# q and k stacked through a DRAM scratch, and the linear bias of the second block added by VectorE

## What is computed

```python
h = relu(layernorm(x))
q, k, v = h @ Wq.T, h @ Wk.T, h @ Wv.T + bv              # 12 heads of 32
scores = q . k * 384**-0.5 + (adj + adj)                  # rows of zeros only are masked
x = x + softmax(scores) v @ Wo.T + bo
h = relu(layernorm(x))
for l in range(2):
    u = h W_left[l] h^T (on and above the diagonal), h W_right[l] h^T (below), / sqrt(384)
    d = exp(u) * adj
    attention = d / (sum(d, axis=2) + 1e-10)
    h_lin = h @ W_lin[l].T + b_lin[l]
    ctx = attention @ h_lin
    h = relu(norm(ctx) * ln_a[l] + ln_b[l])
x = x + h
```

## Time and profile before

| | |
|---|---|
| median of 3 runs | 1622.85 us (1622.07 to 1628.5) |
| the profiled execution | 1625.41 us, span of its core 1623.7 us, mean granted TensorE clock 0.98 |
| busy of the span | PE 96%, PEld 94%, DVE 71%, ACT 57%, POOL 28% |
| last chain by engine | PE 87%, SyncE's queue 7%, DVE 2% |
| transfers | 76.19 MB, 116769 packets; q and k: 768 of 48 KB |
| one turn in the middle | 47.9 us |

### The profile page before, as it was taken

One profiled execution on the slowest core, in us unless ns is written; L12 is line 12 of the kernel. 1 busy time (PEld: TensorE's weight loads), 2 busy tenths in 40 slices (PEclk: granted clock), 3 DMA queues, 4 the chain that ended last, 5 costly groups with the idle time before them and its releaser, 6 DMA issues.

```text
span 1623.7 us, 39352 instructions
## 1 busy us (share of the span) xinstructions
PE 1550.8 (96%) x13888; PEld 1524.4 (94%) x13888; DVE 1146.9 (71%) x4303; ACT 922.7 (57%) x2155; POOL 457.1 (28%) x928
## 2 busy tenths in 40 slices
PE   3699999999999999999999999999999999999984
PEld 3699999999999999999999999999999999999974
DVE  5567777777777677776767777767777776777643
ACT  4456655566665566665556656555666655665632
POOL 4113222333232223322233323222332323332222
PEclk8789999999999999999999999999999999999996
DMA  6101112211112211112221111221111222111100
GB/s 212 40 21 41 43 50 54 53 44 31 47 44 50 54 50 30 42 44 50 53 54 43 33 45 44 50 53 50 33 40 42 53 50 53 46 30 46 31 11 20
DMA packets 116769, 76.19 MB, mean 47 GB/s; under 512 B 14282, under 2 KB 116432, under 8 KB 116576
## 3 DMA queue, kind: packets, MB, share of 16 engines
q1 hardware_dynamic: 116128, 73.06, 17.6%
q0 software_dynamic: 448, 0.60, 0.1%
HBM read 23.28 MB, written 12.58 MB: 22 GB/s over the span
## 4 chain that ended last, share of the span: by engine, by line
PE 87%; SPq 7%; DVE 2%; issue 1%; ACT 1%; DMA 1%; POOL 1%; DVEq 0%; ACTq 0%; POOLq 0%
PE bank L341 70%; SPq L297 6%; PE bank L417 5%; PE bank L347 4%; PE bank L410 3%; PE bank L401 3%; PE bank L423 1%; DMA k<-qk 1%; PE bank L435 0%; ACT prob L506 0%; DVE qk L599 0%; ACT qk L482 0%; SPq L304 0%; DMA x_sb<-x 0%; DVE weights L575 0%
## 5 line engine op out<-in xcount | busy, mean ns | idle before, releaser
L341 PE MATMUL bank<-h,weights 128*128 128x256 f32 x3456 | 429.9, 282 | 5.8 <-DVE h L740 5.1
L341 PEld LDWEIGHTS bank<-h,weights 128*128 128x128 f32 x3456 | 412.0, 190 | 6.7 <-issue 5.7
L506 ACT ACTIVATE prob<-prob,rmin 128x128 f32<-128x128 f32 x768 | 237.2, 404 | 49.9 <-DVE rmin L657 49.9
L341 PE MATMUL bank<-weights,h 128*128 128x384 f32 x1152 | 223.5, 338 | 0.0
L341 PE MATMUL bank<-hA,weights 128*128 128x256 f32 x1728 | 218.5, 283 | 1.4 <-DVE hA L599 1.4
L599 DVE TENSOR_TENSOR n<-bank,n 128x512 fp32r<-128x512 f32 x192 | 129.4, 687 | 122.8 <-ACT n L482 122.7
L341 PEld LDWEIGHTS bank<-hA,weights 128*128 128x128 f32 x1728 | 211.7, 190 | 1.7 <-DVE hA L599 1.7
L341 PEld LDWEIGHTS bank<-weights,h 128*128 128x128 f32 x1152 | 194.1, 188 | 0.0
L482 ACT ACTIVATE n<-bank 128x512 fp32r<-128x512 f32 x192 | 111.9, 606 | 113.9 <-PE bank L341 113.9
L657 DVE CUSTOM_DVE_ANT_0 prob<-bank,adj_sb 128x128 f32<-128x128 f32 x768 | 175.0, 287 | 0.2 <-issue 0.2
L482 ACT ACTIVATE qk<-bank 128x512 f16<-128x512 f32 x96 | 57.2, 595 | 170.5 <-PE bank L341 170.5
(11 more groups left out here) (107 smaller groups left out, 2652.2 us busy)
## 6 DMA issues: line engine op xcount, KB each, us to landing
q<-qk SPq DMA_DIRECT2D x384, 48.0 KB, 1.9
k<-qk SPq DMA_DIRECT2D x384, 48.0 KB, 2.0
x_sb<-x SPq DMA_DIRECT2D x32, 384.0 KB, 3.5
out<-x SPq DMA_DIRECT2D x32, 384.0 KB, 2.5
adj_sb<-adj SPq DMA_DIRECT2D x32, 128.0 KB, 2.1
prob<-w SPq DMA_DIRECT2D x4, 576.0 KB, 6.3
x<-w SPq DMA_DIRECT2D x3, 576.0 KB, 4.4
pT<-w SPq DMA_DIRECT2D x3, 576.0 KB, 5.4
```

The source lines that it names most:

```text
L341: mm = pe.matmul(out, lhsT, rhs, start=(n == 0), stop=(n == len(pairs) - 1))
L506: e = act.activation(prob[:, j, h, :], prob[:, j, h, :], ACT.Exp, bias=rmin[:, j, h:h + 1], scale=-1.0)
```

## The change

**q and k.** A tensor in DRAM (`qk_parts`, two groups deep) takes the place of the copies inside SBUF. After each of QK0, QK1 and QK2 SyncE stores 256 KB (steps qs0 to qs2). Then q3 and k3 load three transfers each of 192 KB, 32 partitions x 4 rows of 1536 bytes. In q3 and k3 the heads lie in another order. The normed x of the next group now waits for the stores (`s_qs`), not for the loads.

**The linear bias.** The matmul with b_lin goes from HL; V keeps its own. The steps C00 to C11 of VectorE are new: a copy of the row sum, the `sums` instruction (moved here from gst), and c_sb = b_lin * row sum + bank. The statistics read c_sb, z0 works from c_sb to c_sb, and z1 as before. ScalarE's copies c1_0 and c1_1 of the second layer go. HTa and HTb wait for z0 by semaphores of their own.

**Order and banks.** All five lists and the banks are written anew, and the turn is cut at another place.

```diff
-                for a in range(HC):
-                    for r, part in enumerate(parts):
-                        sp.dma_start(dst[D * r:D * r + D, a:NH:HC, :], qk[D * a:D * a + D, part, first:first + C, :]).then_inc(s, 16)
+                for r, part in enumerate(parts):
+                    heads = qk_dram[p, :, part, which * C:which * C + C, :].rearrange("(a d) c t -> d a (c t)", d=D)
+                    sp.dma_start(dst[D * r:D * r + D, :, :].rearrange("d (a c) t -> d a (c t)", a=HC), heads).then_inc(s, 16)
...
+                elif step[:2] == "qs":
+                    k = int(step[2])
+                    ge(sp, s_q3, STACKED * (g - 1))
+                    ge(sp, s_k3, STACKED * (g - 1))
+                    wait_drained(sp, f"QK{k}", g)
+                    sp.dma_start(qk_dram[p, :, :, 2 * k:2 * k + 2, :], qk[:, :, 2 * k:2 * k + 2, :]).then_inc(s_qs[k], 16)
...
-                    rows(step, g, w_lin(l), (h0, h1)[l], j, bias=1 + l)
+                    rows(step, g, w_lin(l), (h0, h1)[l], j)
...
-                    wait_drained(pe, "C00", g)
-                    wait_drained(pe, "C01", g)
+                    for j in range(G):
+                        pe.wait_ge(s_z0[j], g + 1)
...
-                    ge(act, s_q3, STACKED * g)
-                    ge(act, s_k3, STACKED * g)
+                    for k in range(3):
+                        ge(act, s_qs[k], 16 * g)
...
-                elif step[:3] == "c1_":
-                    j = int(step[3])
-                    act.wait_ge(s_gst[1][j], g + 1)
-                    act.activation(c_sb[:, j, :], bank(f"C1{j}")[:, 0:H], ACT.Copy).then_inc(free(f"C1{j}"), 1)
...
-                    act.activation(c_sb[:, j, :], bank(f"C0{j}")[:, 0:H], ACT.Identity, bias=shift["gnn"][:, j:j + 1],
-                                   scale=scale["gnn"][:, j:j + 1]).then_inc(free(f"C0{j}"), 1)
+                    act.activation(c_sb[:, j, :], c_sb[:, j, :], ACT.Identity, bias=shift["gnn"][:, j:j + 1],
+                                   scale=scale["gnn"][:, j:j + 1]).then_inc(s_z0[j], 1)
...
+                    wait_filled(dve, job, g)
+                    dve.tensor_copy(dsum[:, j:j + 1], bank(job)[:, H:H + 1]).then_inc(s_dsum[l][j], 1)
+                    dve.tensor_scalar(sums[:, j:j + 1], bank(job)[:, H:H + 1], SUM_EPS, GNN_EPS, ALU.add, ALU.mult)
+                    dve.wait_ge(s_dsum[l][j], g + 1)
+                    dve.scalar_tensor_tensor(out=c_sb[:, j, :], in0=bl_all[:, l, :], scalar=dsum[:, j:j + 1], in1=bank(job)[:, 0:H],
+                                             op0=ALU.mult, op1=ALU.add).then_inc(free(job), 1)
...
     "SP": [
-        ("out", -2), ("q3", 1), ("ld_x", 2), ("k3", 1), ("ld_adj", 2)],
+        ("k3", 1), ("ld_adj", 2), ("out", -1), ("qs0", 2), ("qs1", 2), ("qs2", 2), ("ld_x", 3), ("q3", 2)],
```

More of the change, by code:

```diff
@@ L71 @@
 BANK = {
-    0: ["OT1", "WO1", "V0", "HL10", "C10", "N01", "AT", "HL01"],
-    1: ["PV1", "QK1", "N10", "S00", "S11", "P01", "P10"],
-    2: ["C00", "HTb", "T2a", "P00", "PV0", "OT0"],
-    3: ["WO0", "N12", "T2b", "S01", "P02", "P11"],
-    4: ["T1b", "V1", "U1", "S12", "C11", "P12"],
-    5: ["T1a", "C01", "N00", "U0"],
-    6: ["HTa", "S02", "N02"],
-    7: ["QK0", "QK2", "N11", "HL11", "S10", "HL00"],
+    0: ["S02", "C10", "N01", "P10", "C01", "V0"],
+    1: ["N10", "S00", "S12", "C11", "AT", "OT0"],
+    2: ["N12", "S01", "S10", "HL00", "QK1"],
+    3: ["HL11", "P00", "P11", "PV1", "QK2"],
+    4: ["HL10", "P01", "PV0", "HL01", "C00", "HTa"],
+    5: ["T2a", "N00", "U0", "T1b", "OT1", "WO1", "V1"],
+    6: ["N11", "U1", "N02", "P12", "WO0", "HTb"],
+    7: ["T2b", "S11", "P02", "T1a", "QK0"],
 }
@@ L153, in build @@
         bias_rows = sb("bias_rows", [P, H], F32R)
[L154 removed]
+        pick = sb("pick", [P, P], F32R)
+        bl_all = sb("bl_all", [P, L, H])
         bo_all = sb("bo_all", [P, H])
@@ L200, in build @@
         minus_one = sb("minus_one", [P, G])
-        sums = sb("sums", [P, G])
+        row_sums = sb("row_sums", [P, 2, G])
+        sums, dsum = row_sums[:, 0, :], row_sums[:, 1, :]
         carrier = sb("carrier", [P, 4 + G * C])
@@ L214, in build @@
         s_q3, s_k3 = sem("q3_in"), sem("k3_in")
+        s_qs = [sem(f"qk_out{k}") for k in range(3)]
         s_exp = [[sem(f"exps{j}{c}") for c in range(C)] for j in range(G)]
@@ L226, in build @@
         s_z = [sem(f"normed{j}") for j in range(G)]
+        s_z0 = [sem(f"normed_first{j}") for j in range(G)]
+        s_dsum = [[sem(f"delta_sum{l}{j}") for j in range(G)] for l in range(L)]
         s_h1hi = {ab: sem(f"h1_hi_{ab}") for ab in "ab"}
@@ L239, in build @@
         SPLIT_AFTER = {
-            "ACT": {"": (0,), "xn1_1": (1,), "T1b": (2, 3), "QK0": (4, 5), "QK1": (6,), "V1": (7,), "QK2": (8,), "V0": (9,)},
+            "ACT": {"": (0,), "xn1_1": (1,), "T1b": (2, 3), "QK0": (4, 5), "QK1": (6,), "QK2": (7,), "V1": (8,), "V0": (9,)},
             "DVE": {"ln1_ag": (0,), "T1b": (1, 2), "QK0": (3, 4), "QK1": (5,), "QK2": (6, 7), "V1": (8,), "V0": (9,)}}
@@ L359, in project, with rows @@
                 mm.then_inc(full(job), 1)
-            def rows(job, g, m, h, j, bias=None):
+            def rows(job, g, m, h, j, bias=False):
                 need(m, g)
                 pairs = [(h[:, a, c, j * P:(j + 1) * P], W[:, m, b, c, :]) for c in range(C) for a, b in PARTS]
-                if bias is not None:
+                if bias:
                     if g == 0:
                         pe.wait_ge(s_const, 1)
-                    pairs.append((pick[:, bias, :], bias_rows[:, :]))
+                    pairs.append((pick[:, :], bias_rows[:, :]))
                 split_mm(bank(job)[:, 0:H], pairs).then_inc(full(job), 1)
@@ L393, in run @@
                     wait_drained(pe, "T1b", g)
-                    rows(step, g, WV, hA, int(step[1]), bias=0)
+                    rows(step, g, WV, hA, int(step[1]), bias=True)
                 elif step[0] == "S":
@@ L399, in run @@
                     for a in range(HC):
-                        h = c * HC + a
-                        mm = pe.matmul(bank(step)[:, a * P:(a + 1) * P], q3[:, h, j * P:(j + 1) * P], k3[:, h, j * P:(j + 1) * P], start=True, stop=True)
+                        mm = pe.matmul(bank(step)[:, a * P:(a + 1) * P], q3[:, a * C + c, j * P:(j + 1) * P], k3[:, a * C + c, j * P:(j + 1) * P], start=True, stop=True)
                     mm.then_inc(full(step), 1)
@@ L625, in run @@
                     aggregate(k).then_inc(s_aggr[k], 1)
+                elif step[0] == "C":
+                    l, j = int(step[1]), int(step[2])
+                    job = f"C{l}{j}"
+                    if l == 0:
+                        ge(dve, s_gn[1], g)
+                        ge(dve, s_y[j], g)
+                        if g == 0:
+                            dve.wait_ge(s_cload, 16 * CONST_LOADS)
+                    wait_filled(dve, job, g)
[4 more added lines that the diff above has]
+                                             op0=ALU.mult, op1=ALU.add).then_inc(free(job), 1)
                 elif step[:3] == "gst":
                     l, j = int(step[3]), int(step[4])
[L628 to L632 removed]
+                    wait_drained(dve, f"C{l}{j}", g)
+                    dve.bn_stats(stats["gnn"][:, j, :], c_sb[:, j, :]).then_inc(s_gst[l][j], 1)
                 elif step[:3] == "gag":
```

51 lines of the change are left out of this document (22 added, 29 removed), and 38 rows, old and new, of the table ORDER.

## The result

| | before | after |
|---|---|---|
| median | 1624.3 us (4 runs) | 1611.62 us (4 runs, 1610.95 to 1613.42) |
| ratio after / before | | 0.9917, 95% interval 0.9895 to 0.9939 |
| profiled execution, its span | 1625.4, 1623.7 | 1610.95, 1608.7 |
| clock over the span, profiled | | 0.978 |
| one turn in the middle | 47.92 | 47.59 |

What follows compares the result with a forecast made beforehand. TensorE's work was taken to bound the middle of the run. Terms -21.8 + 20.1 - 2.3 - 11 + 3.9 = -11.1 us took the profiled 1625.4 to 1614.3, or 1612 us on the median; range 1594 to 1636.

Steps and rivals of the forecast that it cites:

- bias matmuls: In HL on TensorE, 128 bias matmuls go, 0.17 us each on its path: -21.8 us.
- wait ahead of HT: TensorE waits for z0, which follows ScalarE's copy of QK2: 0.67 us in 30 turns, +20.1 us.
- q and k in the middle: Nine transfers replace 24 copies a turn, so TensorE's waits for the last copies vanish mid-run: -2.3 us.
- start: First scores of groups 0 and 1 come 5 and 6 us earlier: -11 us, bounds 5 and 15.
- end: Three norms behind C with nothing beside them lay VectorE's path bare, 1.3 us each: +3.9 us.
- VectorE's path: C00 through VectorE and GpSimd to z0: added copies and sums lengthen it by 1.25 us up to the aggregate.
- both would end together: ScalarE's and VectorE's paths to z0 end within 0.04 us, ScalarE's later, so neither can be mended alone.
- VectorE's slack: At C00 VectorE has 1.16 us of slack before the change and some 0.7 us after.
- rival (b): VectorE comes late to C00; each 0.7 us beyond its slack costs 21 us over 30 turns: 1633, chance 0.18.
- the work fits: VectorE's added load, at most 2.9 us a turn, fits, by a count of its steps from U1.m to PV1.o.
- Landing 5 us ahead of S00: Mid-run, x, q and k loads land at 844.7 us, before S00 at 850, so they are hidden.
- Rival (d): The loads land 3 us after S00 is due, in 31 turns: 1700 us, chance 0.06.

Runs made afterwards that it cites:

- experiment 3: Kernel before with q and k through the DRAM scratch and HL's 128 bias matmuls left out, second block's bias not added: 1590.89 us, ratio 0.9792.
- experiment 4: Changed kernel with a bias matmul put back into each HL, VectorE's sum with the bias kept: 1636.76 us, ratio 1.0071.
- experiment 2: Kernel before with only the DRAM scratch for q and k, all else and the order kept: 1614.55 us, ratio 0.9938.
- experiment 7: Changed kernel with z0 ahead of QK2's copy on ScalarE, and WO1 and ln2_st ahead of VectorE's part of QK2: 1615.36 us, ratio 0.9939.
- experiment 8: Changed kernel without VectorE's copy of the row sum, the scalar read from the PSUM bank: 1609.8 us, ratio 0.991.
- experiment 10: Changed kernel with z0 on two engines, the second graph's made by VectorE ahead of its part of QK2: 1594.03 us, ratio 0.9815.
- experiment 9: Changed kernel with three unread VectorE statistics passes over a constant added ahead of C00 in each turn: 1629.84 us, ratio 1.0027.
- experiment 5: Kernel before with only the linear bias moved to VectorE, 24 copies and old order kept: 1672.31 us, ratio 1.0292.
- experiment 6: Kernel before with both the scratch and VectorE's bias, in the old order and banks: 1663.12 us, ratio 1.0227.
- experiment 12: Changed kernel with z0 on two engines and without the copy of the row sum: 1591.89 us, ratio 0.980.

## Why the prediction was right, step by step

| term, us | predicted | measured |
|---|---|---|
| bias matmuls | -21.8 | -23.7 and -25.1 (experiments 3, 4) |
| wait ahead of HT | +20.1 | +22.3 in the loads, about +18.5 net |
| q and k in the middle | -2.3 | -5.5 (experiment 2, between the profiles) |
| start | -11 | -9.9 (7 to 10 over seven profiles) |
| end | +3.9 | +4.9 |
| sum | -11.1 | -15.0 between the spans, -12.7 between the medians |

The mechanism was right: the matmuls' time comes back in full, and the new wait ahead of HT takes most of it. That the forecast lies within 1 us of the median is luck. The term for q and k in the middle was less than half of what it measured, start and end took part of the difference back, and the medians lie closer together than the two profiled executions.

**Bias matmuls.** The term was 2 to 3 us too small. One costs 0.185 to 0.196 us, and the distance in the earlier trace rows was 0.17. In experiment 4 the four HL steps themselves grow by 0.17 or 0.18 each (in the loads' timeline, from HL's first load to the next step's), 0.70 in a turn that is 0.76 us longer; the other 0.05 is spread over the other steps.

**The wait ahead of HT.** The chain was met link by link. ScalarE's copy of QK2 starts 0.31 us behind WO1's first load (predicted 0.31), z0 0.55 behind that (0.50), the pair takes 1.31 (1.33), HT's load comes 0.11 behind its end (0.07), so the gap is 0.74 and not 0.67. Against that, HT's six loads take 0.64 us once they have waited, and 0.75 when they follow at once: net 0.62 to 0.63 a turn. VectorE's path: from the first instruction on C00 to the aggregate 2.59 us, 1.29 more than the earlier trace rows (predicted 1.25). That both would end together, and that neither alone could be mended, is what experiments 7 and 8 show, and experiment 10 shows what takes both away. Only the order was the other way round: ScalarE was predicted to be the later by 0.04 us, and it is the shift, by 0.05. The Trainium skill ("VectorE: DVE Perf Modes", The DRAIN you can't avoid) would have the added instructions count in full, 1.44 us or more; the rows above speak against it (the copy lasts 0.16 us and the next starts 0.07 behind it, the sum lasts 0.62 and the next starts 0.53 behind it). The same section adds that a next instruction that isn't held starts earlier, which fits these rows; the prediction left that out.

**VectorE's slack.** 0.7 us at C00 was predicted, 0.76 measured. Experiment 9 used it up, and the rest went ahead of HT. So rival (b) was a real mechanism, missed by 0.7 us of work a turn. Experiments 5 and 6 show it in the old order, though at other places than C00: it costs the loads 56 us of waits there. My argument that the work fits was right for the new lists and wrong for the old ones: the expectation of experiment 5 (-2 to +2 us) didn't count VectorE's backlog at PV0 and QK2.

**q and k.** Landing 5 us ahead of S00 was predicted; with the median landing it is 5.4, and no score waits in the middle. Rival (d) falls. The term for the middle was mis-sized: it counted what TensorE's busy time lacked, 2.3 us, and took the turn of 47.9 as that of the matmuls. The turn without late copies is 47.73 (experiment 2), so the copies cost 0.19 us a turn, 5.5 us in all. In the kernel before they show in the loads' row (13.6 us of gaps ahead of scores, 9.3 with the scratch). The loads take 4.6 and 5.5 us to land, with six of them and x in flight together. The start was 5 + 6 predicted and 4.0 + 5.9 measured in one execution; the rest of the wait ahead of the first scores remains.

**The turn.** It became 0.33 us shorter; the terms of the prediction give 0.08 (-0.68 + 0.67 - 0.07). Four kernels in a row show where it went: 47.92 before, 47.73 with the scratch (experiment 2), 46.95 without the bias matmuls as well (experiment 3), 47.59 in the changed kernel. That is -0.19, -0.78 and +0.64, and the last is the net wait of 0.62 to 0.63 with all else that the new order and VectorE's bias bring. The next table is worked out from the loads' timelines of these kernels, turns between 300 and 1450 us: the distance from a row's start to the next row's, added up by tile, mean of one turn (23 or 24 turns). Only what moved by 0.05 or more is shown.

| loads of | before | experiment 2 | experiment 3 | after |
|---|---|---|---|---|
| bias_rows (before, with the gap behind HL11) | 1.39 | 1.23 | 0.35 | 0.35 |
| weights,oT (after, with the wait ahead of HT) | 3.05 | 3.06 | 3.04 | 3.80 |
| weights,h (with the gap behind HL11, once no bias matmul is there) | 6.00 | 6.01 | 6.18 | 6.17 |
| ident,c_sb (HT) | 0.72 | 0.72 | 0.73 | 0.60 |
| hl,dT | 2.11 | 2.11 | 2.11 | 2.01 |
| n,h | 4.30 | 4.30 | 4.30 | 4.41 |
| hA,weights | 6.41 | 6.41 | 6.25 | 6.34 |
| h,weights | 12.56 | 12.54 | 12.61 | 12.58 |
| ident,o_sb | 1.43 | 1.43 | 1.43 | 1.37 |
| k,q | 1.23 | 1.22 | 1.23 | 1.28 |
| whole turn | 47.91 | 47.73 | 46.95 | 47.59 |

The step from the first column to the second is k's late copies, nearly all of it in the first row. The next is the matmuls, with small shifts in their neighbours' rows. In the last, rows two and four are the wait: +0.63. The other differences come with other neighbours and add up to nearly nothing; what each comes from was not settled.

**The end.** +4.9 and not +3.9. In the kernel of experiment 8, which has four copies fewer in each turn, the end is 109.2 us and not 110.5; in that of experiment 12 it is only 0.2 less than in that of experiment 10. So the copies' part of the end is 0.2 to 1.3 us, and the rest of the term wasn't taken apart.

**What offset what.** Middle: 6 us better than predicted, about half of it by q and k, the rest mostly by the matmuls. Start and end: 2 us worse. The two profiled spans are 15.0 us apart, the medians 12.7: the predicted time is nearer to the result than its terms are to theirs.
